# Attention's variance step laid over four row groups of 256 columns

## The reference

```
out = softmax(scores + bias + mask) @ v
out = out @ proj_w + proj_b                    # om: 64 channels per pixel
skip = xin + layer_norm(om, ln1_g, ln1_b)      # mean and variance over the 64 channels of a pixel
layer_norm(t) = (t - mean(t)) * rsqrt(var(t) + 1e-5) * g + b
```

## Time and profile before

| what | us |
|---|---|
| median of 3 runs (lowest, highest) | 788.99 (788.33, 789.17) |
| profiled execution, its own time | 790.13 |
| its span | 788.3 |
| TensorE matmul busy | 673.9 |
| VectorE, ScalarE, GpSimd busy | 510.6, 485.4, 354.6 |

### The profile page before, as it was taken

How to read it: one execution, slowest core, us unless ns; L and a number is a source line. 1 busy time by engine, 2 the same in 40 slices (tenths; PEclk the granted TensorE clock), 3 DMA queues, 4 the chain that set the end, 5 groups by cost and what they waited for, 6 DMA issues and landing times. The chain is left out here.

```text
span 788.3 us, 20928 instructions
## 1 busy us (share of the span) xinstructions
PE 673.9 (85%) x8456; PEld 366.2 (46%) x8456; DVE 510.6 (65%) x989; ACT 485.4 (62%) x963; POOL 354.6 (45%) x441
## 2 busy tenths in 40 slices
PE   3795789999999999999999659999999998749780
PEld 2572455555555545555555323333333366735350
DVE  4794477777777787777778421578778786371181
ACT  3655266777777777777776548877777756624000
POOL 4687446778777777787776530022211223100000
PEclk9667599999999999999999969999999999969955
DMA  9550000000000000000000020121122120020268
GB/s 212 137 126 11 1 2 3 2 2 3 2 3 3 2 3 3 2 3 2 3 2 3 2 56 1 27 55 41 41 54 54 47 62 2 28 74 2 63 191 266
DMA packets 15718, 31.42 MB, mean 40 GB/s; under 512 B 7488, under 2 KB 9284, under 8 KB 15620
## 3 DMA queue, kind: packets, MB, share of 16 engines
q1 hardware_dynamic: 12592, 29.16, 13.7%
q10 hardware_dynamic: 2760, 0.66, 0.5%
q0 software_dynamic: 272, 0.27, 0.2%
HBM read 20.71 MB, written 9.37 MB: 38 GB/s over the span
## 5 line engine op out<-in xcount | busy, mean ns | idle before, releaser
L785 POOL TENSOR_TENSOR sc<-sc,mx 128x512 f32<-128x512 f32 x128 | 133.7, 1044 | 107.7 <-DVE mx L719 107.7
L716 DVE TENSOR_TENSOR sc<-s_ps,bias_tab 128x512 f32<-128x512 f32 x128 | 87.6, 684 | 57.7 <-PE s_ps L527 57.7
L1415 POOL TENSOR_TENSOR square<-xs 128x1024 f32<-128x1024 f32 x16 | 34.1, 2134 | 164.0 <-DVE xs L1157 164.0
L538 PE MATMUL t_ps<-consts,sc 128*128 128x128 f32 x512 | 84.9, 289 | 15.8 <-ACT pt L650 12.5
L538 PEld LDWEIGHTS t_ps<-consts,sc 128*128 128x128 f32 x512 | 54.6, 142 | 90.9 <-issue 55.2
L650 ACT ACTIVATE pt<-t_ps 128x512 f32<-128x512 f32 x128 | 75.5, 590 | 30.5 <-PE t_ps L538 29.4
L719 DVE TENSOR_REDUCE mx<-sc 128x8 f32<-128x512 f32 x128 | 87.8, 686 | 4.4
L1072 ACT ACTIVATE hs<-h_ps,fb1s 128x512 f32<-128x512 f32 x128 | 78.1, 689 | 17.7 <-PE h_ps L981 17.5
L527 PE MATMUL s_ps<-kx,qu 32*64 32x128 f32 x2048 | 72.3, 278 | 3.5 <-DVE kx L740 2.9
L981 PE MATMUL h_ps<-xs,fw 64*128 64x512 f32 x256 | 66.9, 634 | 1.3 <-ACT hs L1072 1.2
L527 PEld LDWEIGHTS s_ps<-kx,qu 32*64 32x64 f32 x2048 | 56.7, 134 | 15.2 <-issue 13.4
(11 more groups left out here) (205 smaller groups left out, 1298.4 us busy)
## 6 DMA issues: line engine op xcount, KB each, us to landing
raw<-in_x_dram SPq DMA_DIRECT2D x32, 256.0 KB, 4.7
xr<-in_x_dram SPq DMA_DIRECT2D x32, 256.0 KB, 3.9
out_dram<-x SPq DMA_DIRECT2D x32, 256.0 KB, 4.1
rec_scratch<-r SPq DMA_DIRECT2D x4, 224.0 KB, 2.5
w<-in_L_conv_W_dram SPq DMA_DIRECT2D x1, 784.0 KB
w<-in_L_conv_W_dram SPq DMA_DIRECT2D x1, 672.0 KB
xs<-rec_scratch SPq DMA_DIRECT2D x16, 28.0 KB
xs<-rec_scratch ACTq DMA_DIRECT2D x16, 28.0 KB
```

What stands on the lines that cost most here:

```text
L538: last = pe.transpose(t_ps[:, m], sc[n % KEPT][:, m].rearrange("c h k -> c (h k)"), ident)
L716: dve.tensor_tensor(sc[n % KEPT][:, :, :, :], s_ps[j][:, :, :, :], bias_tab[:, j, hp], ALU.add)\
L785: pool.tensor_tensor(v, v, mx[n % KEPT][:, :].unsqueeze(2).broadcast_to([128, 8, TOK]), ALU.subtract)\
```

## The change

`variances` now makes four matmuls of 256 columns in place of two of 512: tile 0's first and second half go to output rows 0 to 31 and 32 to 63, tile 1's to 64 to 95 and 96 to 127. Logarithm and exponential run over 128 rows of 256 columns. `spread_rstd` multiplies blocks of 64 rows (two groups) with a new constant, `spread_half`, whose part `h` is zero on the rows of the other half; it makes four matmuls of 256 columns in place of two of 512. The constant is built by VectorE at the start of the attention stage, with four memsets and four copies of 32 x 128, ahead of the bias table. The first `spread_rstd` waits for the semaphore of the bias table. `rv` and `spread_half` together take the room that `rv` took.

```diff
-            rv = sb(stage, "rv", [C, COLS])
+            rv = sb(stage, "rv", [128, COLS // 2])
+            spread_half = sb(stage, "spread_half", [128, 2, 128])
...
-                    for j in range(2):
-                        last = pe.matmul(n_ps[rows(j), :], mean_rows, csq[j][:, :], start=True, stop=True)
+                    for g in range(4):
+                        half = slice(256 * (g % 2), 256 * (g % 2 + 1))
+                        last = pe.matmul(n_ps[rows(g), 0:256], mean_rows, csq[g // 2][:, half], start=True, stop=True)
...
                     pe.wait_ge(s["rstd"], p + 1)
+                    if p == 0:
+                        pe.wait_ge(s["table"], 1)
...
-                    for j in range(2):
-                        last = pe.matmul(spread_bank(p, j), spread_image[rows(j)], rv[rows(j), :], start=True, stop=True)
+                    for h in range(2):
+                        for j, (lo, hi) in enumerate(HALVES):
+                            last = pe.matmul(spread_bank(p, j)[:, 256 * h:256 * (h + 1)], spread_half[lo:hi, h], rv[lo:hi, :],
+                                             start=True, stop=True)
...
-                    act.activation(rv[:, :], n_ps[0:C, :], ACT.Ln, bias=eps[0:C, 0:1]).then_inc(s["var_ln"], 1)
+                    act.activation(rv[:, :], n_ps[:, 0:256], ACT.Ln, bias=eps[:, 0:1]).then_inc(s["var_ln"], 1)
...
             def bias_table(dve):
 
+                for g in range(4):
+                    dve.memset(spread_half[rows(g), 1 - g % 2], 0.0)
+                    dve.tensor_copy(spread_half[rows(g), g % 2], spread_image[rows(g)])
                 dve.wait_ge(bias_in, 32)
```

## The result

The changed kernel took 781.83 us (median of 4, 780.42 to 783.88) against 789.08 (4 runs, 788.33 to 789.45) for the one before: ratio 0.9909, 95% interval 0.9891 to 0.9927. Two later measurements of the same pair on other occasions gave 0.9896 (0.9878 to 0.9915) and 0.9896 (0.9875 to 0.9918). The gain is 7 to 8 us; 6.5 was forecast, with 782.5 as the time. One execution of the second measurement took 1575 us, twice the others, and is counted nowhere.

The account below looks back on a forecast made before the run. TensorE's list was taken to bound the attention stage's steady step; -5.6 - 0.6 - 1.3 + 1.0 = -6.5 us, from 788.99 to 782.5. The forecast's own range was 780.0 to 785.2, with rivals 779.8 to 787.0.

Parts of the forecast that it names:

- TensorE's list sets the steady step: Attention stage, pairs 0 to 12: variances' pitch falls from 0.98 to 0.55 us, 13 x 0.43 = 5.6 us gained.
- The spread stays at 1.06: Spread matmuls: blocks of 64 rows run side by side, added weight loads stay hidden, time unchanged at 1.06 us.
- Slack of the query squares: GpSimd's query squares ahead of `norms`: slack falls from 0.67 to 0.24 us, and the 0.14 hand-over just fits.
- Pair 13: 0: Pair 13: variances wait for GpSimd and score 2 for VectorE, so shorter variances gain 0.
- Pair 14: -0.6: Pair 14's chain: 0.15 us from the matmul and 0.22 from each of two ScalarE operations, 0.6 gained.
- Pair 15: -1.3: Pair 15, at half clock: 0.87 us from the matmul and 0.44 from ScalarE, 1.3 gained.
- The stage's start: +1.0: Attention stage's start: bias table instructions, delayed by eight short ones, slow GpSimd's squares; 1.0 us lost, between 0 and 1.6.
- The clock: ±1.5: Half-clock stretches at the attention stage's start and end may shift, about ±1.5 us, not in the sum.
- Rival A: Steady step: GpSimd takes over as bound, a step gains perhaps 0.2 us; net -3.5, 785.5 us; chance 0.11.
- C: Variances: halves of one `csq` tile are not read side by side, pitch stays 0.98; 789.1 us; chance 0.04.
- B: Spread: weight reloads exposed, 0.36 us per spread; net -0.7, 788.3 us; chance 0.05.
- D: Spread: the two 64-row blocks run one after another, 0.86 us more per step; +7.3, 796.3 us; chance 0.03.

Follow-up runs that it names:

- r1: Changed kernel with each of the four variance matmuls issued twice: 787.94 us, ratio 0.9984 to the kernel before.
- r6: Changed kernel with the four spread matmuls ordered tile by tile in place of alternating tiles: 781.93 us, ratio 0.9894 to the kernel before.
- r4: Changed kernel with variance matmuls of only 128 columns, so its output is not the layer norm's: 780.04 us, ratio 0.9882 to the kernel before.
- r5: Kernel before with only the eight VectorE instructions building `spread_half` added ahead of the bias table, read by nobody: 788.68 us, ratio 0.9989.
- r0: Changed kernel again, no edit, for a closer interval and a second profile: 782.15 us, ratio 0.9896 to the kernel before.
- r3: Changed kernel with `spread_half` built in the group norm stage and the first spread's wait on the bias table removed: 783.97 us, ratio 0.993 to the kernel before.
- r10: Changed kernel with `spread_half` built behind the bias table, after the norms of pair 0: 783.38 us, ratio 0.9925 to the kernel before.
- r2: Changed kernel with logarithm and exponential back over 512 columns, TensorE's part as changed: 780.57 us, ratio 0.9887 to the kernel before.

## Why the prediction was right, step by step

- **TensorE's list sets the steady step.** Shown: 0.41 us off the list gave steps of 22.03 in place of 22.44, and r1 gave them back. 22.04 was forecast. The 13 steps together brought 5.0 us and not 5.6: the group's pitch is 0.57 and not 0.55, and two steps are longer than the others. From norms of pair 9 to those of pair 10 it is 22.3 us in all three profiles of the changed kernel, and the step after it takes 22.1 to 22.3. In both the projection group took longer, 1.33 to 1.37 us in the first and 1.17 to 1.37 in the second in place of 1.09, with no wait named:

```profile
284.04 1.37 PE L575 MATMUL a_ps<-ob,wp 64*64 64x512 f32 x8
```

  In the two profiles of before no projection group takes over 1.12 us. One of them has a step of 22.75, but there the 0.31 us stand ahead of the keys' group (L464). So some 0.3 to 0.6 us of the shortfall belong to the changed kernel and repeat; what they are was not tested.
- **The spread stays at 1.06.** Right. By the rule that I weighed (the Trainium skill, TensorE: Matmul & The Clock Gate, "The mechanism") loads to rows in use are not hidden. The changed kernel has twice the loads, all to such rows, and its spread is not longer: 1.06 us. The section makes one exception, for loads into a background buffer of weights; no run here shows whether that is what happens. The same section has matmuls strictly in order; r6, whose blocks of one tile stand one behind the other in the list, has a pitch of 1.07 and so shows no cost of the order.
- **Slack of the query squares.** Right, and near the edge: 0.25 us were left, and r4 showed the hand-over at 0.10.
- **Pair 13: 0.** Right: from norms of pair 15 to the spread of pair 13 it is 19.6 us in both.
- **Pair 14: -0.6.** Measured -0.75: ScalarE's two operations brought the 0.44 that was taken for them, the matmul 0.32 and not 0.15.
- **Pair 15: -1.3.** Measured -1.68; the matmul was at the full clock and fell by 1.27, not by the 0.87 of the sum. That 0.4 is the clock's and was not foreseen.
- **The stage's start: +1.0.** Measured +0.65 at norms of pair 0. The eight short instructions took 1.9 us, above the bound of 1.8 that was put to them, so more of the table met the squares. I had GpSimd lose a third of a microsecond at three meetings; there were four, at 0.16 each. VectorE lost most, 3.4 us on eight instructions, and its table ended at 76.3 where the forecast had it near 74. The Trainium skill (SBUF — State Buffer, "Who interferes with whom") has the engine that issues first keep the shared ports for its whole instruction, and the other blocked. That fits VectorE here, whose additions took 1.26 us each, about as long as a square (1.22). It does not fit GpSimd: a whole addition let in between two squares would cost 0.35, and the square lost 0.16. By norms of pair 2 the cost is within the scatter of that start: 50.7 to 50.9 us after the first matmul, against 50.1 and 50.7 before, and r5 shows no cost in the time at all.
- **The clock: ±1.5.** The prediction said that the stretches at half clock may shift, left the sign open and put nothing into the sum. In r0's expectation I then took the shift for chance, and that was wrong: it follows the kernel. All three profiles of the changed kernel have the -1.45 ahead of pair 14 and a longer rest, +1.0 in the mean. The two nearly cancel, and they lie inside the bound that was given.

Sum: -5.0 - 0.75 - 1.68 + 0.65 - 1.45 + 1.0 = -7.2, against 7.25 measured first. The stretch from norms of pair 0 to pair 2, which differs by 0.2 within its scatter, and the first stage are left out of it. That the forecast's total came within 1 us is in part luck: the steady part fell short of it by 0.6, and the last pairs, the start and the clock made up for that with 0.5, 0.35 and 0.45. One bound of its own range was added up wrongly: 782.5 + 1.0 + 1.5 is 785.0, not 785.2.

Rival A would have shown norms waiting, C a pitch of 0.98, B and D a longer spread; none did.

## What to carry to other kernels

Matmuls that fill only part of the output's row groups are worth trying spread over all of them (here 0.98 to 0.57 us). The time saved counts in full where the timeline shows the engine's groups end to end; look then for the input with the least slack, since it says how much more there is to gain. Setup work is not free because its own engine is idle: ask which engine it slows down, and whether that one is on the path at that moment. Then ask whether the cost is larger than the scatter of the stretch it falls in: two attempts to win back 0.65 us here (r3, r10) won nothing. At the ends of a stage, read the granted clock too: a gain of a microsecond there was offset behind it in r2.

## What the runs showed of the hardware

- Two 64-row blocks ran side by side whether their matmuls alternated in the list or stood tile by tile (pitch 1.06 and 1.07 to 1.08).
- Four blocks of 256 columns, on four column groups of 32 and two to each tile, had a pitch of 0.57 us; two blocks of 512 had 0.98.
- Eight weight loads of 64 x 128 ahead of passes of 256 columns cost no more than four of 32 x 128 ahead of 512 (a spread of 1.06 to 1.07 us against 1.06).
- Eight VectorE additions of 128 x 256, both inputs in SBUF, took 2.77 us alone and 6.15 beside four GpSimd squares, which took 4.72 in place of 4.08; the same to 0.01 us in two kernels. One addition ran with each square, at 1.26 us in place of 0.42.
- From the spread of pair 13 to the variances of pair 14 the time was the same, to 0.2 us, in each repeated profile of a kernel: 13.21 to 13.23 us at full clock in three of the changed kernel, 14.75 and 14.58 with a part at half clock in two of before. Over eight profiles with steps of 22.03 it held while the stage's start varied by 4 us. What sets it is open.
